# Half of the first recurrence's row tiles summed on TensorE instead of VectorE, and the chunk loop written out straight

## The reference

```python
# block 1, a state-space mixer, per sequence; DI = 512 channels, 16 states
h = rmsnorm(x); xi, z = split(h @ in_proj.T); xi = silu(causal_conv4(xi))
dt, B, C = split(xi @ x_proj.T); delta = softplus(dt @ dt_proj.T + b); A = -exp(A_log)
for t in range(L):                                       # "the recurrence"
    s = s * exp(delta[t] * A) + delta[t] * B[t] * xi[t]   # s: 512 channels x 16 states
    y[t] = sum over the 16 states of s * C[t]
out = ((y + xi * D) * silu(z)) @ out_proj.T + x
# block 2: attention with 8 heads over 2 x 64 context rows, rotary tables, softmax, then a 256x256 layer
# block 3: a shared expert and 8 routed experts (top 2), each silu(x @ W1 + b1) * (x @ W3 + b3) @ W2 + b2
```

## Time and profile before

| | us |
|---|---|
| median of 3 runs (lowest, highest) | 1202.07 (1201.78, 1212.36) |
| the profiled execution's own time | 1197.24 |
| its span, first to last instruction | 1195.1 |
| TensorE busy in it (share of the span) | 916.2 (77%) |
| VectorE busy | 848.5 (71%) |
| GpSimd busy | 537.0 (45%) |
| ScalarE busy | 530.0 (44%) |
| mean granted TensorE clock, 1.0 being 2.4 GHz | 0.816 |

### The profile page before, as it was taken

The page is one execution under the profiler, slowest core; times in us unless marked ns, Lnnn a source line. Parts: engine busy times, 40 slices in busy tenths (PEclk is TensorE's granted clock), DMA queues, the critical chain, the costliest instruction groups (busy, mean ns, idle before and its releaser), DMA issues.

```text
span 1195.1 us, 13820 instructions
## 1 busy us (share of the span) xinstructions
PE 916.2 (77%) x3960; PEld 692.5 (58%) x3960; DVE 848.5 (71%) x1255; ACT 530.0 (44%) x995; POOL 537.0 (45%) x319
## 2 busy tenths in 40 slices
PE   4845558667689998578689999577789994767996
PEld 2434445256477785266477875266577782644885
DVE  1699996578999965579899964589899961212333
ACT  3533443644456524644445525554446522322442
POOL 1266640363457830453467830553467823001552
PEclk9955559877779999788679998787679997665998
DMA  5110100111023311111023301111023203000331
GB/s 198 37 35 36 53 1 36 72 36 63 18 72 124 88 36 55 71 36 63 18 80 116 96 28 55 71 36 63 19 81 131 90 17 114 1 0 16 118 117 34
DMA packets 38254, 72.61 MB, mean 61 GB/s; under 512 B 3871, under 2 KB 12712, under 8 KB 38174
## 3 DMA queue, kind: packets, MB, share of 16 engines
q1 hardware_dynamic: 38174, 71.65, 18.3%
HBM read 65.14 MB, written 2.30 MB: 56 GB/s over the span
## 4 chain that ended last, share of the span: by engine, by line
PE 35%; issue 24%; DVE 22%; POOL 11%; ACT 5%; DVEq 1%; POOLq 0%; DMA 0%; ACTq 0%; SPq 0%
PE ps L887 8%; DVE hs L1071 8%; POOL dbu L533 6%; PE ps L964 5%; DVE yacc L1123 4%; PE ps L743 4%; PE ps L861 4%; PE ps L816 3%; DVE work L1235 2%; PE ps L822 2%; POOL work L568 2%; POOL work L550 2%; PE ps L794 2%; PE ps L801 1%; PE ps L906 1%
## 5 line engine op out<-in xcount | busy, mean ns | idle before, releaser
L533 POOL TENSOR_TENSOR dbu<-v,bbc 128x1024 f32<-128x1024 f32 x128 | 303.0, 2373 | 233.6 <-DVE v L1057 127.8
L1071 DVE TENSOR_TENSOR_SCAN hs<-ps,carry,dbu 128x512 f32<-128x512 f32 x256 | 312.9, 1265 | 2.0 <-PE ps L743 1.5
L639 ACT ACTIVATE ps<-delta,neg_a 128x512 f32<-128x512 f32 x256 | 175.3, 692 | 208.6 <-DVE hs L1071 208.2
L743 PE MATMUL ps<-ident,hs 128*128 128x128 f32 x1024 | 186.1, 340 | 89.2 <-DVE yacc L1123 74.3
L743 PEld LDWEIGHTS ps<-ident,hs 128*128 128x128 f32 x1024 | 156.4, 179 | 118.7 <-DVE hs L1071 74.5
L1123 DVE SCALAR_TENSOR_TENSOR yacc<-ps,ctok,yacc 128x512 f32<-128x512 f32 x240 | 167.2, 737 | 1.2 <-PE ps L743 1.0
L560 POOL TENSOR_TENSOR w_lo<-w13s,w_hi 128x512 fp32r<-128x512 f32 x72 | 93.0, 1292 | 133.7 <-ACT w_hi L718 131.9
L964 PE MATMUL ps<-w2s,work 128*128 128x256 f32 x576 | 137.2, 381 | 0.3
L887 PE MATMUL ps<-x_hi,w_hi 128*128 128x512 f32 x288 | 109.7, 463 | 9.2 <-DVE work L1241 8.8
L964 PEld LDWEIGHTS ps<-w2s,work 128*128 128x128 f32 x576 | 106.5, 191 | 15.1 <-DVE work L1241 1.5
L1235 DVE SCALAR_TENSOR_TENSOR work<-work 128x512 f32<-128x512 f32 x72 | 81.6, 1133 | 45.6 <-POOL work L568 44.7
(11 more groups left out here) (164 smaller groups left out, 1240.9 us busy)
## 6 DMA issues: line engine op xcount, KB each, us to landing
w13s<-in_w SPq DMA_DIRECT2D x72, 256.0 KB, 2.7
bbc<-brow_dram SPq DMA_DIRECT2D x32, 512.0 KB, 3.8
w2s<-in_w SPq DMA_DIRECT2D x36, 256.0 KB, 2.6
cbc<-comb_dram SPq DMA_DIRECT2D x32, 256.0 KB, 3.4
work<-work SPq DMA_DIRECT2D x16, 256.0 KB, 2.3
xn<-in_x SPq DMA_DIRECT2D x5, 512.0 KB, 4.8
xt<-in_x SPq DMA_DIRECT2D x4, 512.0 KB, 3.7
rope<-in_rope_q SPq DMA_DIRECT2D x4, 512.0 KB, 4.2
```

What stands on the lines that cost most here:

```text
L533: pool.tensor_tensor(dbu[:, i % DRING, :, :], v[:, 2 * h:2 * h + 2, :], bbc[:, n // 2 % 2, n % 2, :].rearrange("p (o t) -> p o t", o=1) .t ...
L639: act.activation(ps[:, unit % 2, :], delta[:, q, :], ACT.Exp, scale=neg_a[:, q * NS + m:q * NS + m + 1]).then_inc(da_done.sem, 1)
L743: last = pe.transpose(ps[:, bank, t * P:(t + 1) * P], src(t), ident[:, :])
L1071: dve.tensor_tensor_scan(hs[:, m % 2, q, 0:TC], ps[:, unit % 2, :], dbu[:, n % DRING, q % 2, :], carry[:, m, q:q + 1], ALU.mult, ALU.add). ...
```

## The change

1. `sum_states` on VectorE takes only the even tile of each step in chunk 0.
2. The odd tile is scaled by C on ScalarE (`scale_states`, at the `sum` step, into one of the two halves of `x1t`).
3. TensorE sums the scaled tile (`sum_on`): four matmuls with the scaled tile as weights and the identity as the moving operand, so that each both turns the tile back and adds it, into banks 4 to 7, one bank to a block of channels. They stand a step after the scaling, ahead of that step's transposes.
4. In `post` 0 of chunk 0 only the even tiles of `yacc` are turned (8 transposes instead of 16), and L1077 (now with bank 4 + q) reads banks 4 to 7.
5. The odd transposes wait for the scaling (`scaled_done`) instead of VectorE's sum.
6. `schedule()` now writes out all five bodies with their chunk numbers, and `streams` just walks it: no loop, no chunk register. The fetch of chunk 4 and TensorE's wait for it are gone; SyncE's wait before the rotary table of chunk 3 is for another signal.

```diff
-            with eng.Fori(1, CHUNKS, 1) as i:
-                body(i, False, False)
-            body(CHUNKS, False, True)
+            for stream, chunk, kind, step in SCHEDULE:
+                if stream == "mixer":
+                    mixer(chunk, kind, step)
+                else:
+                    second(chunk, step, kind)
...
+                if kind == "sum" and 3 <= n < 2 * NS + 3 and is_first(j):
+                    scale_states(n - 3)
...
+            def scale_states(i):
+
+                n, half = divmod(i, 2)
+                t = 2 * half + 1
+                act.wait_ge(*ht_ps.at(0, n * NT + t + 1))
+                act.wait_ge(*ctok_done.at(0, 1))
+                if i >= 2:
+                    act.wait_ge(summed.sem, i - 1)
+                act.activation(x1t[:, half, :], ps[:, 3, :], ACT.Copy, scale=ctok[:, t, n:n + 1]).then_inc(scaled_done.sem, 1)
...
+                if kind == "scan" and 4 <= n and is_first(j):
+                    sum_on(n - 4)
                 if kind == "scan" and 2 <= n < 2 * NS + 2:
                     state_rows(j, *divmod(n - 2, 2))
                 if kind == "post" and n == 0:
+                    if is_first(j):
+                        sum_on(2 * NS - 1)
+                        pe.wait_ge(*y_done.at(0, NS * NT))
+                        for q in range(Q):
+                            for t in range(0, NT, 2):
+                                last = pe.transpose(ps[:, 4 + q, t * P:(t + 1) * P], yacc[:, t, q * P:(q + 1) * P], ident[:, :])
+                            last.then_inc(yt_ps.sem, 1)
+                        return
...
+            def sum_on(i):
+
+                n, half = divmod(i, 2)
+                t = 2 * half + 1
+                if i == 0:
+                    pe.wait_ge(kv_done.sem, 2)
+                pe.wait_ge(scaled_done.sem, i + 1)
+                for q in range(Q):
+                    last = pe.matmul(ps[:, 4 + q, t * P:(t + 1) * P], x1t[:, half, q * P:(q + 1) * P], ident[:, :],
+                                     start=(i == 0), stop=(n == NS - 1), skip_group_check=True)
+                last.then_inc(summed.sem, 1)
...
                     pe.wait_ge(*scan_done.at(j, Q * (n + 1)))
-                    pe.wait_ge(*y_done.at(j, max(0, n * NT + t - 1)))
+                    if is_first(j) and t % 2:
+                        pe.wait_ge(scaled_done.sem, 2 * n + half)
+                    else:
+                        pe.wait_ge(*y_done.at(j, max(0, n * NT + t - 1)))
...
             def sum_states(j, n, half):
 
-                for t in range(2 * half, 2 * half + 2):
+                for t in (2 * half,) if is_first(j) else (2 * half, 2 * half + 1):
```

More of the change, by code:

```diff
@@ L69, in schedule, with mixer, second @@
 def schedule():
-    tick = lambda t: [("early", t), ("mid", t), ("late", t)]
-    steps = [("setup", 0), ("pre", 1), ("post", 3), ("post", 4), ("pre", 2), ("post", 5), ("pre", 3)] + tick(0)
-    steps += [("pre", 4), ("pre", 5), ("early", 1), ("pre", 6), ("late", 1), ("setup", 1)]
-    for t in range(2, PRE_TICKS):
-        steps += tick(t)
-    for s in range(SCAN_TICKS):
-        t = PRE_TICKS + s
-        steps += [("early", t), ("sum", s), ("mid", t), ("scan", s), ("late", t)]
-        if SCAN_TICKS - 12 <= s < SCAN_TICKS - 8:
-            steps.append(("fetch", s - SCAN_TICKS + 12))
-    for k, t in enumerate(range(PRE_TICKS + SCAN_TICKS, T_OUT + 1)):
-        steps += [("post", k)] if k < 3 else []
-        steps += tick(t)
+    steps = []
+    for i in range(CHUNKS + 1):
+        def mixer(chunk, *what):
+            return [("mixer", chunk, *what)] if 0 <= chunk < CHUNKS else []
+        def second(t, parts=("early", "mid", "late")):
+            return [("second", i - 1, p, t) for p in parts] if i else []
+        if i == 0:
+            for n in range(4):
+                steps += mixer(0, "fetch", n)
+            steps += mixer(0, "setup", 0)
+        steps += mixer(i, "pre", 1) + mixer(i - 1, "post", 3) + mixer(i - 1, "post", 4)
+        steps += mixer(i, "pre", 2) + mixer(i - 1, "post", 5) + mixer(i, "pre", 3)
+        steps += second(0)
+        steps += mixer(i, "pre", 4) + mixer(i, "pre", 5)
+        steps += second(1, ("early",)) + mixer(i, "pre", 6) + second(1, ("late",))
+        if i == 0:
+            steps += mixer(0, "setup", 1)
+        for s in range(SCAN_TICKS):
+            t = PRE_TICKS + s
+            steps += second(t, ("early",)) + mixer(i, "sum", s) + second(t, ("mid",)) + mixer(i, "scan", s)
+            steps += second(t, ("late",))
+            if SCAN_TICKS - 12 <= s < SCAN_TICKS - 8:
+                steps += mixer(i + 1, "fetch", s - SCAN_TICKS + 12)
+        for k, t in enumerate(range(PRE_TICKS + SCAN_TICKS, T_OUT + 1)):
+            if k < 3:
+                steps += mixer(i, "post", k)
+            steps += second(t)
     return steps
@@ L282, in block_kernel @@
         y_done = signal("y_done", NS * NT)
+        scaled_done, summed = one("scaled_done"), one("summed")
         yt_ps = signal("yt_ps", Q)
@@ L356, in streams @@
         def streams(eng, mixer, second):
-            def body(i, first, last):
-                for kind, step in SCHEDULE:
-                    if kind in ("early", "mid", "late"):
-                        if not first:
-                            second(i - 1, step, kind)
-                    elif kind == "post" and step >= 3:
-                        if not first:
-                            mixer(i - 1, kind, step)
-                    elif kind == "setup":
-                        if first:
-                            mixer(i, kind, step)
-                    elif kind == "fetch" and not last:
-                        mixer(i + 1, kind, step)
-                    elif not last:
-                        mixer(i, kind, step)
-            for step in range(4):
-                mixer(0, "fetch", step)
-            body(0, True, False)
-            with eng.Fori(1, CHUNKS, 1) as i:
-                body(i, False, False)
-            body(CHUNKS, False, True)
+            for stream, chunk, kind, step in SCHEDULE:
[3 more added lines that the diff above has]
+                    second(chunk, step, kind)
         @block.sync
@@ L972, in _ @@
             streams(pe, mixer, second)
-            pe.wait_ge(*xn_done.at(CHUNKS, 1))
         @block.vector
@@ L1119, in sum_states @@
                         dve.wait_ge(*xz_ps.at(j, 2 * Q))
-                        dve.tensor_scalar(yacc[:, t, :], ps[:, 2 + t % 2, :], c, None, ALU.mult).then_inc(y_done.sem, 1)
+                        dve.tensor_scalar(yacc[:, t, :], ps[:, 2 + t % 2, :], c, None, ALU.mult).then_inc(y_done.sem, add)
                     else:
```

11 lines of the change are left out of this document (8 added, 3 removed).

## The result

The changed kernel takes 1169.41 us (median of four runs, 1167.59 to 1170.56), the one before 1201.92 (four runs, 1199.26 to 1212.36): a ratio of 0.9725, with an interval of 0.9665 to 0.9786. Forecast were 1178.5 us, in a range of 1170 to 1190. The sign and the main part came as forecast, but the time lies 9.1 us under the forecast and 0.6 under the range. Between the two profiled executions (1197.24 and 1168.82) the gain is 28.4 us, against 23.6 summed: these 4.8 us are what this part looks for. The other 4.8 are the distance of before's median from its profiled execution, which the forecast carried over; after's median lies only 0.6 above its own execution.

A forecast was written before the change was run, and what follows sets the result against it. VectorE was taken to bound the first recurrence, with branch idle at the loop's edges; -19.0 + 1.5 + 0.6 - 0.3 - 3.3 - 3.1 = -23.6 us from the 1202.07 us median gave 1178.5 us, range 1170 to 1190.

The forecast's parts named there:

- The first recurrence: Chunk 0's recurrence: one VectorE sum leaves each step, period 3.67 to 3.01 us; -17.2 us with its smaller terms.
- two steps at half clock, 1.5 us lost: First recurrence: the new order's first two steps run at half clock with TensorE needing 3.78 us each; +1.5 us.
- The fetch's two bursts: First recurrence: ScalarE's 1.69 us fetch bursts fall between an exp and the scaling; 0.3 us each, +0.6 us.
- the way from there to L1117: End of the first recurrence, last sum to the first L1077: 6.43 us becomes about 6.1 at full clock; -0.3 us.
- The edges: Passes 1 to 2 and 2 to 3: straight order removes the branch's idle, input product starts earlier; -3.3 and -3.1 us.
- The fetch of chunk 4 was on ScalarE under TensorE's expert products, 0: Third pass: dropping the fetch of chunk 4 saves nothing, as it lay under TensorE's expert products; 0 us.
- the loop cost more than its edges: Rival: loop registers may delay waits in each of three passes, 2 or 3 us in sum; 1171 us, chance 0.07.
- The clock didn't swing: Rival, first recurrence: clock swings, half the steps at 3.78 us; 1188 us, chance 0.13 shared with a late ScalarE.
- ScalarE's exps: Rival, first recurrence: ScalarE reaches the next exp 0.3 us late each step; 1188 us, chance 0.13 shared with clock swing.
- The gap went: Rival, pass edges: the 2 us idle stays or equal fetch stalls appear elsewhere; 1185 us, chance 0.08.
- the low clock: Rival, first recurrence: clock never rises, TensorE bounds at 3.78 against 3.67 us a step; 1199.5 us, chance 0.04.
- a slower TensorE: Rival, first recurrence: clock stays low and matmuls take 0.35 us, 4.74 us a step; 1227 us, chance 0.04.

The follow-up runs named there:

- e3: The changed kernel with the fetch of the non-existent chunk 4 put back, still in straight order: 1172.01 us.
- e4: The changed kernel with the fetch's ScalarE squares and copies given one to a step instead of in two bursts: 1166.48 us.
- e6: The changed kernel with only the load and ScalarE's squares and copies of the fetch for chunk 4 added: 1170.86 us (one execution).
- e1: The kernel before with only the new first recurrence, keeping the hardware loop and the fetch of chunk 4: 1177.55 us, ratio 0.9785.
- e9: The changed kernel with all fetches moved from scan steps 23 to 26 to steps 0 and 2 to 4 of the recurrence: 1169.84 us.
- e10: The changed kernel with GpSimd's product dbu made for half its columns while expert products run beside the recurrence: 1166.65 us (one execution).
- e12: The changed kernel with the fetch spread one operation to a step and moved to the first 12 steps of the recurrence: 1164.68 us.
- e2: The kernel before with only the straight order, without the fetch of chunk 4, VectorE summing both tiles: 1187.57 us, ratio 0.9867.
- e5: The changed kernel with the first recurrence's odd tiles neither scaled nor summed, their transposes kept: 1166.28 us (one execution).
- e7: The changed kernel with only VectorE's mean and GpSimd's pow of the fetch for chunk 4 added: 1177.51 us (one execution).

## Why the prediction was right, and where it failed

**The first recurrence**, -17.2 forecast, -17.7 measured. The period of 3.01 us came to the digit. The scaling takes 0.67 us (0.69 taken), the added group at half clock 1.91 us at 71.49 (1.84 taken), at full clock 1.06 in length and 0.9 in pitch (0.96 taken). The clock read 1.00 from 80 us on. The forecast's "two steps at half clock, 1.5 us lost" didn't occur: scans follow at 3.01 us from 72.53 to 75.54, though TensorE's clock was at half until 74.3 us: the group at half clock held up nobody else. The fetch's two bursts made steps of 3.40 and 3.45 us, 0.39 and 0.44 us lost where 0.3 was booked for each. By the last sum of the scans (157.01 against 175.67) 18.7 us were won, where the steps of the forecast give 16.9; the way from there to L1117 is 5.89 us instead of 6.43, -0.5 against -0.3. Against that stands a cost that the forecast left out: after the recurrence the granted clock fell (0.88 between 168 and 176), and the output product took 8.53 us,

```profile
166.90 8.53 PE L842 MATMUL ps<-wout,v 128*128 128x256 f32 x32
```

where e3, e4 and e6, with the same work, take 7.3 from its start to its end and have their first input product at 173.7 to 173.9 (in e1, e9, e10 and e12 it takes 8.3 to 8.8 us as well). The two errors, 1.8 us one way and 1.5 the other, nearly cancel, so it is in part luck that this term fits.

**The edges**, -6.4 forecast, -7.4 measured with the rest of passes 1 and 2. That it is the loop is shown by e2, with the straight order alone (262.29 and 262.50 us), and by e1, where the loop stays, the passes are 265.79 and 264.32 and the idle of 2.12 and 1.76 us is still there. The Trainium skill's account of a taken branch (Runtime: NRT & Kernel Launch, section Instruction fetch mechanics), which the prediction cited, agrees: the idle of 2 us is gone with the branch. That the fetch of instructions fills it, and not the registers of the loop, no run shows by itself.

**The step that failed** is "The fetch of chunk 4 was on ScalarE under TensorE's expert products, 0". It measured 3.0 us between the two kernels and 3.3 by e3. The reason was wrong in kind: it asked whether ScalarE had room beside TensorE, and ScalarE had. What the fetch costs is a push that lays GpSimd's product over VectorE's, and TensorE then waits for VectorE, 1.63 and 1.66 us in e3. It could have been read before, from the group of `gm` by its extremes and from TensorE's waits:

```profile
L1235 DVE SCALAR_TENSOR_TENSOR work<-work x72: 664/708/2858, 347.8 to 1179.2; 128x512 f32<-128x512 f32 x72
...
919.58 0.74 PE L887 MATMUL ps<-x_hi,w_hi 128*128 128x512 f32 x2 [1.65 <-DVE work L1241]
...
926.90 0.73 PE L887 MATMUL ps<-x_hi,w_hi 128*128 128x512 f32 x2 [1.66 <-DVE work L1241]
```

Its two longest in the third pass of before, at 915.88 and 923.20, stand behind the fetch of a chunk that nobody uses, and each of the two waits follows one of them.

**The rival "the loop cost more than its edges", 1171 us,** gave nearly the right number by the wrong mechanism. It wanted registers that delay waits in each pass; e3 has no loop and its third pass is as long as before, and passes 1 and 2 have only what the edges explain.

**The other rivals fell.** The clock didn't swing in the recurrence (0.98 on average from 83 to 155, with one fall of 3.4 us at 139.1). ScalarE's exps came 0.12 us after the scans. The gap went. Neither the low clock nor a slower TensorE was seen.

**The rest of the miss** is the base. I put the sum on a median that lies 4.8 us above the execution from which all durations came, and the 25 executions of the kernel before in all sets of runs take from 1192.04 to 1212.36, while no straight version scattered by more than 4 us (e1, with the loop, by 4.2). Why the kernel before varies so much wasn't tried. The interval of +-4 us was too narrow for it. The time lies only 0.6 us under the range, so that putting right either alone, the fetch's 3.0 us or the base's 4.8, would have brought a range of the same width over it.

## What to carry to other kernels

Work that is hidden under a busy engine can still cost: ask what it delays on the queues of the others, and what these then run on top of. Where VectorE sets the pace and has an operation with both inputs in SBUF, look at the shortest and the longest duration of that one line; a spread like the one from 0.66 to 2.80 us here is a reason to look at what GpSimd runs beside the long ones, and a mean hides it. And when a sum moves from the engine that bounds to TensorE, count the gain by VectorE's period alone: the added matmuls lifted the clock here and stayed hidden, but the lifted clock gave nothing on top (e5 has the same 3.01 us at 0.50).

## What was unexpected in the hardware

`gm` on VectorE takes 0.66 to 0.69 us alone and 2.80 beside a GpSimd product of 2.38 us, and 1.68 when the GpSimd instruction is halved to 1.28. In all 36 cases of the changed kernel in which GpSimd was first, it ends 0.54 to 0.56 us after GpSimd's instruction.

The granted clock of one stretch of the recurrence, 88 to 120 us, is 0.50 in e5 and 1.00 in the changed kernel. There it had risen at 74.3 us, behind 4 us in which TensorE was busy throughout:

```profile
70.00:72.00 2.00, 2.00 (x11) 1.93 (x11) 2.00 (x3) 1.09 (x2) 1.47 (x1) 0.50 0.00 0
72.00:74.00 2.00, 2.00 (x11) 2.00 (x11) 2.00 (x3) 1.45 (x3) 1.88 (x1) 0.50 0.00 0
...
88.00:120.00 32.00, 23.25 (x176) 19.36 (x174) 32.00 (x32) 21.51 (x37) 25.14 (x11) 1.00 0.15 51
```

And the same code meets more than one course of the clock: a fall at 168 us that e3 doesn't have (1.5 us), one in pass 2 of e9 (3 us), one in the last part of e7 and e10 (5 us). At the first no edit tells the two kernels apart up to there; at the others the edits stand in other parts, and whether their shifts set it off isn't shown. These falls limit how closely such a time can be forecast.
